# A fused FFN with three LoRA products: another order of the step, one send moved to ScalarE's queue, x split in halves

## The reference

```
gate = x @ Wg.T + lora(x, A_gate, B_gate) * 0.5          # 512 -> 1376
up   = x @ Wu.T + lora(x, A_up,   B_up)   * 0.5
act  = silu(gate) * up
down = act @ Wd.T + lora(act, A_down, B_down) * 0.5      # 1376 -> 512
x1   = x + down @ sign(W0).T + b0
out  = x1 + ffn1(cond1(x1))     # linear: one 16-row table per adapter, + b1
```

## Time and profile before

| | |
|---|---|
| three runs | 978.22, 982.28, 982.3 us (median 982.28) |
| the profiled execution | 983.49 us, its span 981.6 us |
| PE busy | 927.7 us, 95% of the span |
| PEld busy | 711.9 us |
| DVE / ACT / POOL busy | 430.1 / 167.8 / 93.4 us |
| PE's granted clock | 0.994 of 2.4 GHz over the span |
| DMA | 135.23 MB, 138 GB/s in the mean |

### The profile page before, as it was taken

How to read it: one execution, slowest core, us unless ns; L and a number is a source line. 1 busy time by engine, 2 the same in 40 slices (tenths; PEclk the granted TensorE clock), 3 DMA queues, 4 the chain that set the end, 5 groups by cost and what they waited for, 6 DMA issues and landing times.

```text
span 981.6 us, 28045 instructions
## 1 busy us (share of the span) xinstructions
PE 927.7 (95%) x10528; PEld 711.9 (73%) x10528; DVE 430.1 (44%) x1018; ACT 167.8 (17%) x287; POOL 93.4 (10%) x81
## 2 busy tenths in 40 slices
PE   9989999899999999999999999999999999999998
PEld 6867777677777777777777677777767777777675
DVE  5743434444343443444344444443443444344443
ACT  6731111101111111111111101111111111111101
POOL 1110110110111001001110110111001001110111
PEclk9989999999999999999999999999999999999999
DMA  9924544554554445445444454554445445444542
GB/s 353 369 64 119 135 107 124 134 137 122 139 138 115 134 123 142 129 127 143 124 124 128 136 136 120 142 140 114 133 123 143 128 128 143 121 126 127 138 113 68
DMA packets 166678, 135.23 MB, mean 138 GB/s; under 512 B 55680, under 2 KB 138368, under 8 KB 166528
## 3 DMA queue, kind: packets, MB, share of 16 engines
q1 hardware_dynamic: 111568, 109.22, 39.3%
q10 hardware_dynamic: 54144, 22.57, 8.9%
q0 software_dynamic: 944, 3.15, 0.8%
HBM read 92.11 MB, written 11.01 MB: 105 GB/s over the span
## 4 chain that ended last, share of the span: by engine, by line
PE 93%; issue 5%; DMA 1%; POOL 0%; SPq 0%; DVE 0%; ACT 0%
PE gu_ps L772 51%; PE y_ps L816 27%; PE gu_ps L904 4%; PE out_ps L837 3%; PE out_ps L872 2%; PE y_ps L772 1%; PE out_ps L826 1%; PE gu_ps L895 1%; PE out_ps L772 1%; PE out_ps L847 1%; DMA b_rows<-in_btab 0%; DMA lb_raw<-in_lbw 0%; POOL b_rows L408 0%; PE gu_ps L934 0%; PE gu_ps L1005 0%
## 5 line engine op out<-in xcount | busy, mean ns | idle before, releaser
L772 PE MATMUL gu_ps<-wg_sb,xT_sb 128*128 128x512 f32 (+1 forms) x1152 | 261.7, 372 | 42.8 <-issue 42.8
L816 PE MATMUL y_ps<-down_sb,actT_sb 128*128 128x512 f32 x1056 | 269.8, 403 | 0.0
L772 PEld LDWEIGHTS gu_ps<-wg_sb,xT_sb 128*128 128x128 f32 x1152 | 205.8, 189 | 84.6 <-issue 56.4
L816 PEld LDWEIGHTS y_ps<-down_sb,actT_sb 128*128 128x128 f32 x1056 | 191.7, 189 | 91.1 <-issue 51.6
L772 PE MATMUL gu_ps<-wu_sb,xT_sb 128*128 128x512 f32 (+1 forms) x1152 | 252.6, 368 | 2.7 <-DMA b_rows<-in_btab 2.7
L772 PEld LDWEIGHTS gu_ps<-wu_sb,xT_sb 128*128 128x128 f32 x1152 | 207.1, 188 | 33.1 <-issue 3.1
L568 DVE TENSOR_TENSOR actT_sb<-landed,actT_sb 128x512 fp32r<-128x512 f32 (+1 forms) x96 | 72.0, 750 | 241.6 <-ACT actT_sb L424 240.6
L424 ACT CAST actT_sb<-landed 128x512 fp32r<-128x512 f32 (+1 forms) x96 | 56.0, 584 | 432.6 <-DMA landed<-act_sb 275.2
L586 DVE TENSOR_TENSOR act_sb<-act_sb,gu_ps 128x512 f32<-128x512 f32 (+1 forms) x94 | 58.1, 618 | 118.8 <-ACT act_sb L435 118.8
L609 DVE STREAM_TRANSPOSE lhs_sb<-t_own 32x32 f32<-32x32 f32 x512 | 103.9, 203 | 7.7
L435 ACT ACTIVATE act_sb<-gu_ps 128x512 f32<-128x512 f32 (+1 forms) x96 | 49.7, 552 | 324.2 <-PE gu_ps L895 302.7
(11 more groups left out here) (134 smaller groups left out, 419.7 us busy)
## 6 DMA issues: line engine op xcount, KB each, us to landing
b_rows<-in_btab SPq DMA_DIRECT2D x128, 216.0 KB
ad_raw<-in_adtab SPq DMA_DIRECT2D x128, 88.0 KB, 2.1
xT_raw<-in_xT SPq DMA_DIRECT2D x32, 256.0 KB, 3.4
a_raw<-in_atab SPq DMA_DIRECT2D x128, 64.0 KB, 2.0
x_in<-in_x SPq DMA_DIRECT2D x32, 256.0 KB, 2.9
landed<-act_sb ACTq DMA_DIRECT2D x124, 64.0 KB, 2.2
landed<-act_sb SPq DMA_DIRECT2D x124, 64.0 KB, 2.1
x_landed<-x_turn ACTq DMA_DIRECT2D x124, 64.0 KB, 2.3
```

The source lines that it names most:

```text
L772: last = nc.tensor.matmul(o, w, m, start=start and n == 0, stop=stop and n == len(terms) - 1, skip_group_check=not check)
L816: last = nc.tensor.matmul(y_ps[:], actT_sb[:, ACTT_SLOT[c] + n, a, :], down_sb[:, blk, b, :], start=c == 0 and n == 0 and (a, b) == (0, 0) ...
```

## The change

- TensorE's step: `down(prev, 0)` no longer opens it. Up to the first session stand now gate 0, up 0, gate 1, up 1 (before: down 0, gate 0, up 0, gate 1). Between `small` and `first_rows` stand down 1 and down 0 (before: down 1 and up 1). In step 0 the session comes ahead of gate 1.
- The accumulation in `y_ps` opens with chunk 1, but in `finish` with chunk 0 as before.
- Chunk 2's four sends go from SP's queue to ACT's, behind those of chunk 1.
- SP: `load_x(prev)` stands at the head of the step, in the place of the sends, and waits for chunk 1 to be turned; `load_b(g)` follows it.
- `split_xT` works in two halves (pieces 0 and 1, then 2 and 3), each with its own signals.
- Start: POOL clears `b_rows` as soon as the tables are stored, SP loads the B rows of step 0 then; the split of up's chunk 2 on DVE moves behind `turn_small`.
- `finish`: chunk 2's copy from PSUM is DVE's and not ACT's.

The diff without the semaphores' names and the `finish` of ACT and TensorE:

```diff
...
@@ -334,7 +334,10 @@
                              ).then_inc(L["xT_in"], 16)
 
             def load_x(g):
-                after(sp, L["x1_done"], g)
+                if last(g):
+                    sp.wait_ge(L["x1_done"], g)
+                else:
+                    sp.wait_ge(L["act_turned"], g * NC + 2)
                 sp.dma_start(x_in[:], x[bass.ds(g * P, P), :]).then_inc(L["x_in"], 16)
 
             def store(g):
@@ -347,8 +350,8 @@
 
             def step(g, prev, pp, nxt):
                 if prev is not None:
-                    send_act(sp, prev, 2)
-                load_b(g)
+                    load_x(prev)
+                    load_b(g)
                 if nxt is not None:
                     load_xT(nxt)
                     load_a(nxt)
@@ -360,9 +363,9 @@
                 load_ad_sbd(g)
                 if prev is not None:
                     load_c(prev)
+
+            def finish(g):
                 load_x(g)
-
-            def finish(g):
                 sp.wait_ge(L["small_mm"], g + 2)
                 for b in range(GB):
                     at = row_of(1, g, b, R1)
@@ -373,6 +376,8 @@
                 sp.dma_start(out[g * P:(g + 1) * P, :], x1_turn[:]).then_inc(L["stored"], 16)
                 sp.wait_ge(L["stored"], 16 * G)
 
+            sp.wait_ge(S["rows_clear"], 1)
+            load_b(0)
             sp.wait_ge(S["rows_clear"], 2)
             step(0, None, None, 1)
             step(1, 0, None, 2)
@@ -402,10 +407,11 @@
                     table, at = sb_table, n - 8
                 k = n % ROWS_RING
                 pool.dma_start(table[at * P:(at + 1) * P, :], rows_out[:, k, :]).then_inc(rows_free[k], 16)
+            pool.wait_ge(S["sbd_mm"], 2)
+            rows_stored(pool)
+            nc.gpsimd.memset(b_rows[:], 0.0).then_inc(S["rows_clear"], 1)
             pool.dma_start(bias_sb[:], bias).then_inc(S["bias_in"], 16)
             pool.wait_ge(S["down_mm"], NBLK)
-            rows_stored(pool)
-            nc.gpsimd.memset(b_rows[:], 0.0).then_inc(S["rows_clear"], 1)
             nc.gpsimd.memset(cs_rows[:], 0.0).then_inc(S["rows_clear"], 1)
             pool.wait_ge(S["bias_in"], 16)
             add_bias0(0)
@@ -425,8 +431,10 @@
 
             def split_xT(g):
                 act.wait_ge(L["xT_in"], 16 * g + 16)
-                after(act, L["xT_used"], g)
-                copy(xT_sb[:, :, 0, :], xT_raw[:]).then_inc(L["xT_hi"], 1)
+                for half in range(2):
+                    after(act, L["xT_used"], 2 * g - 1 + half)
+                    at = slice(2 * half, 2 * half + 2)
+                    copy(xT_sb[:, at, 0, :], xT_raw[:, at, :]).then_inc(L["xT_hi"], 1)
 
             def silu(g, c):
                 w = CHUNKS[c][1]
@@ -457,6 +465,7 @@
                     silu(prev, 1)
                     silu(prev, 2)
                     send_act(act, prev, 1)
+                    send_act(act, prev, 2)
                     split_actT(prev, 1)
                     split_actT(prev, 2)
                 else:
...
@@ -576,8 +584,10 @@
                 dve.wait_ge(S["dve_step"], steps[0])
 
             def split_xT(g):
-                dve.wait_ge(L["xT_hi"], g + 1)
-                lo(xT_sb[:, :, 1, :], xT_raw[:], xT_sb[:, :, 0, :]).then_inc(L["xT_lo"], 1)
+                for half in range(2):
+                    dve.wait_ge(L["xT_hi"], 2 * g + 1 + half)
+                    at = slice(2 * half, 2 * half + 2)
+                    lo(xT_sb[:, at, 1, :], xT_raw[:, at, :], xT_sb[:, at, 0, :]).then_inc(L["xT_lo"], 1)
 
             def gated(g, c):
                 w = CHUNKS[c][1]
@@ -640,12 +650,12 @@
                     gated(prev, 2)
                     turn_act(prev, 2)
                     split_actT(prev, 1)
-                else:
-                    split_up(2, range(KC))
                 scale_small(g, 0, T_W if prev is None else TD_AT + TD_W if pp is None else SMALL)
                 turn_small(g, (0, 1) if prev is None else (0, 1, 3) if pp is None else (0, 1, 2, 3))
                 if prev is not None:
                     split_actT(prev, 2)
+                else:
+                    split_up(2, range(KC))
                 gated(g, 0)
                 turn_act(g, 0)
                 if pp is not None:
@@ -663,6 +673,9 @@
                     dve.wait_ge(L["silu_done"], g * NC + c + 1)
                     nc.vector.tensor_tensor(to.rearrange("p n (i r) -> p r n i", r=4), by_row(act_sb[c][:]),
                                             by_row(gu_ps[GU_BANK[c][1]][:]), ALU.mult).then_inc(L["act_done"], 1)
+                dve.wait_ge(E["act_tr"], 2)
+                nc.vector.tensor_copy(by_quadrant(landed[2], KC), gu_ps[5][:].rearrange("p (n q t) -> p n q t", n=KC, q=4)
+                                      ).then_inc(E["act_raw2"], 1)
                 split_actT(g, 1)
                 scale_small(g + 1, TD_AT, SMALL)
                 turn_small(g + 1, (2, 3))
@@ -781,14 +794,12 @@
             def gate(g, c, pieces=range(KC)):
                 f, w = CHUNKS[c]
                 if 0 in pieces:
-                    if c == 0:
-                        pe.wait_ge(L["xT_lo"], g + 1)
-                        if first(g):
-                            pe.wait_ge(S["wg_lo"], KC)
+                    if c == 0 and first(g):
+                        pe.wait_ge(S["wg_lo"], KC)
                     if c == 1:
-                        if first(g):
-                            pe.wait_ge(S["down_lo"], NBLK)
                         after(pe, L["silu_done"], g * NC - 1)
+                if c == 0:
+                    pe.wait_ge(L["xT_lo"], 2 * g + (2 if KC - 1 in pieces else 1))
                 product(gu_ps[GU_BANK[c][0]][:, 0:w], [(xT_sb[:, k, a, :], wg_sb[:, b, k, f:f + w])
                                                        for k in pieces for a, b in THREE], None,
                         start=0 in pieces, stop=KC - 1 in pieces)
@@ -797,16 +808,18 @@
                 f, w = CHUNKS[c]
                 if 0 in pieces and first(g):
                     pe.wait_ge(S["wu_lo"], (c + 1) * KC)
+                if 0 in pieces and c == 1:
+                    after(pe, L["act_done"], g * NC - 1)
                 last = product(gu_ps[GU_BANK[c][1]][:, 0:w], [(xT_sb[:, k, a, :], wu_sb[:, b, k, f:f + w])
                                                               for k in pieces for a, b in THREE], None,
                                start=0 in pieces, stop=KC - 1 in pieces)
-                if c == NC - 1 and KC - 1 in pieces:
+                if c == NC - 1 and (1 in pieces or KC - 1 in pieces):
                     last.then_inc(L["xT_used"], 1)
 
-            def down(g, c, blocks=range(4)):
+            def down(g, c, blocks=range(4), begin=1):
                 if 0 in blocks:
                     pe.wait_ge(L["actT_lo"], g * NC + c + 1)
-                    if c == 0:
+                    if c == begin:
                         after(pe, L["x1_done"], g)
                 count = len(CHUNK_BLOCKS[c])
                 for n, blk in enumerate(CHUNK_BLOCKS[c]):
@@ -814,11 +827,10 @@
                         continue
                     for a, b in THREE:
                         last = nc.tensor.matmul(y_ps[:], actT_sb[:, ACTT_SLOT[c] + n, a, :], down_sb[:, blk, b, :],
-                                                start=c == 0 and n == 0 and (a, b) == (0, 0),
+                                                start=c == begin and n == 0 and (a, b) == (0, 0),
                                                 stop=c == NC - 1 and n == count - 1 and (a, b) == (1, 0),
                                                 skip_group_check=True)
-                if c == NC - 1 and count - 1 in blocks:
-                    last.then_inc(L["y_mm"], 1)
+                return last
 
             def t_rows():
                 for k in range(KC):
@@ -851,6 +863,8 @@
 
             def small_ready(g, prev, pp):
                 pe.wait_ge(L["a_in"], 16 * GB * (g + 1))
+                if first(g):
+                    pe.wait_ge(S["down_lo"], NBLK)
                 if prev is not None:
                     pe.wait_ge(L["act_in1"], SENT * g)
                     pe.wait_ge(L["act_in2"], SENT * g)
@@ -907,24 +921,34 @@
                 last.then_inc(L["second_mm"], 1)
 
             def step(g, prev, pp):
-                if prev is not None:
-                    down(prev, 0)
-                gate(g, 0)
-                up(g, 0)
-                gate(g, 1, range(0, 3))
-                small_ready(g, prev, pp)
-                gate(g, 1, range(3, 4))
-                small(prev, pp)
-                if prev is not None:
+                gate(g, 0, range(0, 2))
+                gate(g, 0, range(2, 4))
+                if prev is None:
+                    up(g, 0, range(0, 3))
+                    small_ready(g, prev, pp)
+                    up(g, 0, range(3, 4))
+                    small(prev, pp)
+                    gate(g, 1)
+                    up(g, 1, range(0, 3))
```

(40 more changed lines are left out.)

## The result

The changed kernel takes 1049.32 us (1044.58 to 1050.45, 4 runs), the one before 982.29. The ratio is 1.068, 95% interval 1.064 to 1.073: slower by 67 us, where 971 us was forecast. Its profiled execution has a span of 1046.4 us and a mean granted clock of 0.949 (0.994 before).

The account below looks back on a forecast made before the run. PE's waits for chunk 2 were taken to bound the kernel. 983.5 - 6.3 (start) - 45.4 (old loss) - 0.2 (step 1) + 30 L, with L = 1.35, gave 972.1, less 1.2 for the median: 971 us, range 956 to 984.

Parts of the forecast that it names:

- What bounds the kernel: PE, busy 927.7 of 981.6 us; its waits for chunk 2 before the first session lose 1.62 us a loop step.
- PE's order: More matmuls ahead of the first session's wait; with chunk 2's landing unchanged, wins 0.54 us a step, leaving 1.08.
- Chunk 2's sends on ACT: Sends issue hardly 0.1 us earlier, but SP's B rows come 3 us earlier and collide; loss 1.35 us a step.
- The bounds are 1.9 ... and 3.2 us: Limits for the last chunk 2 send, issue to landing, from all sends seen; loss 0.65 to 1.93 us a step.
- the 2.1 + 0.5: Time taken for chunk 2's last send: 2.1 us as before plus 0.5 for meeting the tail of a B rows burst.
- Rival 3: B rows delay chunk 2 past PE's new place: send 3.2 us, 988 us, slower from 3.0 us on; chance 0.1.
- L = 1.35: Forecast loss in us in each of 30 steps, at PE's wait for chunk 2 before the first session.
- Second session: Its cover shrinks to 18 down matmuls, 4.36 us against 3.85 needed; wait 0 to 0.1 us, taken as 0.
- x in halves: At the step's head, splitting x in halves avoids 0.4 us plus a restart; cost taken as 0, at most 0.2.
- start: Step 0's B rows loaded early: PE's stall and the slow clock behind it go, saving 6.3 us.
- Straight-line steps: Steps 1 and 2, outside the loop, get the loop's loss from ACT's queue: 2.5 us given back.

Follow-up runs that it names:

- the last kernel above: Changed kernel with chunk 2's sends heading SP's step, x, x transposed and lhs copy issued by ACT, C rows loaded in halves: 928.54 us (0.944 against the kernel before).

## Why the prediction was wrong

- *What bounds the kernel*: right. PE's wait for chunk 2 ahead of the first session, 0.35 us from landing to PE, in every kernel here that has the wait.
- *PE's order*: right. With SP's queue as it was the loss is 1.0 us a step (forecast 1.08) and the time 958 us (963).
- *Chunk 2's sends on ACT*: the issue times were right to 0.2 us. **The step that failed is the sentence on the bounds**, "The bounds are 1.9 ... and 3.2 us", and the 2.1 + 0.5 taken between them. The last send took 4.0 us (4.09 in the median, in the trace up to 4.6). The 3.2 was the longest of the sends before, and in the loop none of these had met four loads of 216 KB and x together; it bounded nothing. Landing in the median, by what was beside the sends (the last load of C rows is issued by Z+4.6 in all four, the last send at Z+7.1):

| beside the eight sends | landing | last send | more than the line above |
|---|---|---|---|
| nothing else (x and B rows held) | Z+9.24 | 2.16 | |
| x, 256 KB | Z+9.47 | 2.39 | 0.23 |
| x and half of each B row, 256 + 432 KB | Z+10.44 | 3.30 | 0.97 |
| x and B rows, 256 + 864 KB | Z+11.26 | 4.09 | 0.82 |

- Rival 3 named this mechanism and gave it 0.1; from its own deciding point (3.0 us) it was right, in its size (988 us) wrong, by the same bound.
- *The clock* was missing from the sum altogether: the slow stretch behind the wait was put at nothing, without a reason, and took 1.26 to 1.5 us a step. The earlier trace rows had shown a slow stretch behind a wait of 2.73 us, and I counted it for the start, but not for a wait that might grow. The idle time here is 2.0 to 3.3 us, where a loop step before had 1.46 and a clock of 1.00.
- The bill by periods: a step without any loss takes 26.68 us (the last kernel above), the changed one 30.74. The wait is 2.64 + 0.16 = 2.8 us of the 4.06, the clock the other 1.26 (1.5 by filling the wait). Against L = 1.35 that is 30 x (1.45 + 1.26) = 81 us; forecast and measurement are 78 apart.
- The rule of "DMA: Bandwidth & Descriptors" in the Trainium skill, section "Queues, rings and completion order", by which I let a quarter be held once by one burst of 0.75 us and no longer, did not hold as I read it: the last quarter took 1.9 us longer than with nothing beside it. I had left out that the quarters ahead of the last one could be held too. Whether that is the whole of it, no run here shows.
- *Second session, x in halves, start*: right (no wait; 0.48 us saved where it counts; 5.9 us of 6.3).
- *Straight-line steps*: the sign was right. Step 2 now waits 2.10 us.

## What to carry to other kernels

A DMA queue that is late can be a shelter: SP's late B rows left the DMA engines to the sends that PE waits for. Before a transfer is moved to a quieter issuing engine, ask what the old queue will issue in its place, and keep large loads behind the small transfer that ends on the critical path, by order or by a wait on its landing. A longest time seen in a trace is no upper bound for a meeting that the trace doesn't contain; and when a PE wait may grow, put the lower clock behind it into the sum. And take a delay from many steps: with B rows held, the same landing lay anywhere from Z+9.24 to Z+9.92.

## What the runs showed of the hardware

- The last of eight 64 KB sends between partitions took 2.16 us from issue to landing with no load issued in the 2.5 us ahead of it, 2.39 (2.20 to 2.69) beside a 256 KB load issued 1.3 us ahead of it, and 4.09 (3.36 to 4.67) beside one such load and four of 216 KB issued every 0.95 us; half the bytes of these four took 0.8 us off.
- PE's granted clock stayed 1.00 behind idle times of 1.46 us in each step, fell to a mean of 0.91 of the next 19 us behind 2.68 us, and stayed at 1.00 when 2.3 us of such a wait were filled with matmuls of no use: 45 us of 1049.
- Between these the idle time alone doesn't tell: with B rows halved the clock fell in 10 of 23 steps, in one of them behind 1.74 us, and stayed at 1.00 in another behind 2.02 us.
